# A Transformer layer with routed experts on one core: the experts' second layer by split products, and a score product moved

## The reference, cut to what matters

```python
x = x + attention(layernorm(x), Wq, Wk, Wv, Wo)     # x: 16 x 256 x 128, 16 heads, keys of 8, values of 64, causal
x = x + experts(layernorm(x), gate_w, w1, w2)       # 8 experts, capacity 64 tokens each per batch row

def experts(x, gate_w, w1, w2):
    probs = softmax(x @ gate_w)                      # B, T, 8
    top_p, top_idx = top_k(probs.transpose(0, 2, 1), 64)
    xin = gather(x, top_idx)                         # B, 8, 64, 128
    h = gelu(einsum('BElC,ECH->BElH', xin, w1))      # hidden width 512
    y = einsum('BElH,EHC->BElC', h, w2) * top_p[..., None]
    return zeros.at[b_idx, top_idx].add(y)
```

## Time and profile before

| | us |
|---|---|
| median of 3 runs | 535.61 |
| profiled execution | 535.0 |
| its span | 533.3 |
| PE busy | 512.2 (96%) |
| DVE busy | 422.5 (79%) |
| ACT busy | 401.3 (75%) |
| POOL busy | 264.6 (50%) |

### The profile page before, as it was taken

How to read it: one execution, slowest core, us unless ns; L and a number is a source line. 1 busy time by engine, 2 the same in 40 slices (tenths; PEclk the granted TensorE clock), 3 DMA queues, 4 the chain that set the end, 5 groups by cost and what they waited for, 6 DMA issues and landing times.

```text
span 533.3 us, 13983 instructions
## 1 busy us (share of the span) xinstructions
PE 512.2 (96%) x4783; PEld 424.8 (80%) x4783; DVE 422.5 (79%) x1081; ACT 401.3 (75%) x1379; POOL 264.6 (50%) x252
## 2 busy tenths in 40 slices
PE   3799999999999999999999999999999999999996
PEld 2477787887887877877877877867789998999996
DVE  6878898888888888889989999999974577634444
ACT  3799998999989899898989989899653644434330
...
DMA packets 49447, 45.71 MB, mean 86 GB/s; under 512 B 4208, under 2 KB 46192, under 8 KB 49392
## 3 DMA queue, kind: packets, MB, share of 16 engines
...
## 4 chain that ended last, share of the span: by engine, by line
PE 88%; DVE 5%; issue 2%; ACT 2%; DMA 1%; POOLq 0%; POOL 0%; ACTq 0%; DVEq 0%
PE ctx_ps L1266 16%; PE t_ps L1353 10%; PE misc_ps L1275 10%; PE t_ps L1239 5%; PE t_ps L1249 5%; PE t_ps L1240 5%; PE misc_ps L1177 4%; PE s_ps L1337 4%; PE misc_ps L1178 4%; PE misc_ps L1179 4%; PE s_ps L1225 3%; PE s_ps L1338 3%; PE s_ps L1339 3%; PE s_ps L1212 3%; PE s_ps L1221 2%
## 5 line engine op out<-in xcount | busy, mean ns | idle before, releaser
L580 ACT ACTIVATE prob<-s_ps,neg_max 128x128 f32<-128x128 f32 (+1 forms) x512 | 208.8, 426 | 2.7 <-DVE neg_max L1008 0.5
L504 POOL TENSOR_TENSOR probn<-prob,inv 128x1024 f32<-128x1024 f32 x64 | 121.3, 1895 | 53.0 <-DVE inv L1072 53.0
L580 ACT ACTIVATION_READ_ACCUMULATOR prob<-s_ps,neg_max 128x1 f32 x512 | 108.4, 212 | 0.0
L497 POOL TENSOR_TENSOR probn<-prob,inv 128x512 f32<-128x512 f32 x64 | 66.7, 1042 | 56.4 <-PE t_ps L1249 56.0
L628 ACT ACTIVATE hT<-s_ps 128x512 f32<-128x512 f32 x64 | 38.0, 598 | 64.4 <-PE s_ps L1339 61.8
L1008 DVE TENSOR_REDUCE neg_max<-s_ps 128x4 f32<-128x1024 f32 x63 | 75.1, 1193 | 0.8 <-PE s_ps L1225 0.8
L533 POOL TENSOR_TENSOR y_parts<-y_sb,y_parts 128x512 fp32r<-128x512 f32 x16 | 21.3, 1328 | 106.9 <-ACT y_parts L638 106.9
L1275 PE MATMUL misc_ps<-wo_sb,ctxT 128*128 128x128 f32 x512 | 67.8, 275 | 0.9 <-DVE x_all L827 0.9
L1275 PEld LDWEIGHTS misc_ps<-wo_sb,ctxT 128*128 128x128 f32 x512 | 62.2, 192 | 1.3 <-issue 1.3
L1239 PE MATMUL t_ps<-ident,probn 128*128 128x128 f32 x256 | 61.8, 281 | 0.0
L1240 PE MATMUL t_ps<-ident,probn 128*128 128x128 f32 x256 | 60.1, 275 | 0.0
...
## 6 DMA issues: line engine op xcount, KB each, us to landing
...
```

What stands on the lines that cost most here:

```text
L497: nc.gpsimd.tensor_tensor(probn[r][:, 0:HG * P].rearrange("p (i k) -> p i k", i=HG), prob[r][:, 0:HG * P].rearrange("p (i k) -> p i k", i=HG),
L504: nc.gpsimd.tensor_tensor(probn[r][:, HG * P:].rearrange("p (i k) -> p i k", i=HG), prob[r][:, HG * P:].rearrange("p (i k) -> p i k", i=HG ...
L580: last = nc.scalar.activation(prob[r][:, first + i * keys:first + (i + 1) * keys], scores[:, i, :], ACT.Exp, bias=neg_max[:, r, block_, i: ...
```

## The change: what it does

The second layer is made the other way round. The weights `w2` are now the stationary operand and are held as a pair (`w2_first_hi/lo`, `w2_rest_hi/lo`); the hidden layer is the moving operand (256 columns) and is a pair too (`h_hi`, `h_lo`). `expert_out(m, half)` is 12 fp32r matmuls for one expert of the pair; both halves of a pair fill the bank `misc_ps[1]`. The result stands with the channels on the partitions, so ACT copies it (`copy_y`) and four PE transposes (`turn_y`) turn it back to where it was before.

To get the pair of the hidden layer, ACT evaluates the gelu twice from PSUM, once into `h_raw` (float32) and once into `h_hi`; POOL subtracts for k = 0, 2 and 3 and DVE for k = 1 (`split_h`). The weights' pair is made for the experts 0 to 3 on POOL in the units 47 to 54 (a copy and a subtraction in turn), for the experts 4 to 7 by four ACT copies behind `copy_turned_late(63, 1)` and four POOL subtractions behind `split_w1`.

The loop's order is new: expert_out(n - 1, 1) stands where the whole of it stood, turn_y(n - 1) follows hidden(n, 3), and expert_out(n, 0) ends the step. split_y moves ahead of gelu(n, 1) but for n = 3, 4, 5; scale_y moves behind the rounds of the top-64 search in DVE's list; DVE splits the last y. In the attention units `first_scores` stands ahead of `values`. The stores of the result are written out instead of a loop, and the buffer for DMA descriptors is smaller.

```diff
+Y_SPLIT_AT = {3: 2, 4: 2, 5: 2}
+W2_UNITS = tuple(range(47, 55))
...
+        yT_ps = misc_ps[1][:, :].rearrange("p (h q s) -> p h q s", h=2, q=QB)
...
@@ POOL @@
+            def split_w2(e, step):
+                if step == 0:
+                    pool.wait_ge(w2_loaded, 16)
+                    nc.gpsimd.tensor_copy(w2_first_hi[:, e, :, :], w2_first[:, e, :, :]).then_inc(w2_hi_done, 1)
+                else:
+                    pool.wait_ge(w2_hi_done, e + 1)
+                    nc.gpsimd.tensor_tensor(w2_lo_of(e), w2_raw_of(e), f32(w2_hi_of(e)),
+                                            ALU.subtract).then_inc(w2_ready, 1)
+            def split_h(n, k):
+                pool.wait_ge(h_ready, 4 * n + k + 1)
+                await_count(pool, yT_done, 2 * n - 1 + k // 2)
+                nc.gpsimd.tensor_tensor(h_lo[:, k, :, :], h_raw[:, k % RING, :, :], f32(h_hi[:, k, :, :]),
+                                        ALU.subtract).then_inc(h_lo_ready, 1)
...
+                    if at(u, W2_UNITS):
+                        split_w2(*divmod(u - W2_UNITS[0], 2))
...
-            norm_scale(B - 1)
-            for m in range(B):
-                parts = y_parts[m // QB % RING]
...
+            for e in range(EP, E):
+                split_w2(e, 1)
+            for n in range(B + 1):
+                for k in range(4):
+                    if k == Y_SPLIT_AT.get(n, 1) and has(n - 2, B):
+                        split_y(n - 2)
+                    if n < B and k != 1:
+                        split_h(n, k)
+                    if n == 0 and k == 1:
+                        norm_scale(B - 1)
@@ ACT @@
             def gelu(n, k):
                 act.wait_ge(h_done, 4 * n + k + 1)
-                nc.scalar.activation(hT[n % RING][:, k // 2, 2 * (k % 2):2 * (k % 2) + 2, :],
-                                     h_ps[k % 2], ACT.Gelu).then_inc(h_ready, 1)
+                await_count(act, *((h_lo_ready, 3 * n - 1), (h_lo_ready, 3 * n), (h_lo_ready, 3 * n + 1), (h_lo1_ready, n + 1))[k])
+                nc.scalar.activation(h_raw[:, k % RING, :, :], h_ps[k % 2], ACT.Gelu)
+                await_count(act, yT_done, 2 * n - 1 + k // 2)
+                nc.scalar.activation(h_hi[:, k, :, :], h_ps[k % 2], ACT.Gelu).then_inc(h_ready, 1)
+            def copy_y(m):
+                act.wait_ge(yT_done, 2 * (m + 1))
+                await_count(act, y_done, m - 1)
+                nc.scalar.activation(y_turned[:, m % RING, :, :].rearrange("p q (h s) -> p h q s", h=2),
+                                     yT_ps, ACT.Copy).then_inc(yT_ready, 1)
...
             copy_turned_late(63, 1)
+            for e in range(EP, E):
+                split_w2(e)
             copy_xin(3)
...
-                        if k == 2 and has(m, B):
+                        if k == Y_SPLIT_AT.get(n, 1) and has(m, B):
                             split_y(m)
+                        if k == 2 and has(n - 1, B):
+                            copy_y(n - 1)
                         gelu(n, k)
@@ DVE @@
+            def split_h(n):
+                dve.wait_ge(h_ready, 4 * n + 2)
+                await_count(dve, yT_done, 2 * n - 1)
+                nc.vector.tensor_tensor(h_lo[:, 1, :, :], h_raw[:, 1, :, :], f32(h_hi[:, 1, :, :]),
+                                        ALU.subtract).then_inc(h_lo1_ready, 1)
...
                 for b in GATHERED_AT.get(n, ()):
                     take_gathered(b)
+                if 0 < n < B and n not in GATHERED_AMID:
+                    split_h(n)
...
                 m = n - 1
-                if has(m, B):
-                    scale_y(m)
...
                 for s in TOPS_BEHIND.get(n, ()):
                     top_round(1, s)
+                if has(m, B):
+                    scale_y(m)
+                if m == B - 1:
+                    split_last_y()
@@ PE @@
-            def expert_out(m):
-                pe.wait_ge(h_ready, 4 * (m + 1))
...
-                for q in range(QB):
-                    for c in range(HC):
-                        for half in range(2):
-                            last = nc.tensor.matmul(y_ps[half * CAP:(half + 1) * CAP, q, :],
-                                                    hT[m % RING][:, half, c, q * CAP:(q + 1) * CAP],
-                                                    w2_of(2 * (m % EP) + half)[:, c, :],
+            def expert_out(m, half):
+                e = 2 * (m % EP) + half
+                pe.wait_ge(h_lo_ready, 3 * m + (1, 3)[half])
+                if half == 0:
+                    pe.wait_ge(h_lo1_ready, m + 1)
...
+                for c in range(HC):
+                    hi, lo = [part[:, 2 * half + c // 2, c % 2, :] for part in (h_hi, h_lo)]
+                    for w, h in ((w2_hi_of, hi), (w2_hi_of, lo), (w2_lo_of, hi)):
+                        last = nc.tensor.matmul(misc_ps[1][:, half * QB * CAP:(half + 1) * QB * CAP], w(e)[:, c, :], h,
+                                                start=(c == 0 and h is hi and w is w2_hi_of),
+                                                stop=(c == HC - 1 and w is w2_lo_of))
+                last.then_inc(yT_done, 1)
+            def turn_y(m):
+                pe.wait_ge(yT_ready, m + 1)
...
                 for q in range(QB):
+                    last = nc.tensor.transpose(y_ps[:, q, :], y_turned[:, m % RING, q, :], ident[:, :])
                 last.then_inc(y_done, 1)
...
+                        await_count(pe, filled0, u + 2)
+                        first_scores((j + 2) % G, par if j < 2 else 1 - par)
+                    if has(u + 2, UNITS):
                         w, q = u + 2, (j + 2) % G
...
                         values(q, xb)
-                    if has(u + 2, UNITS):
-                        if j == 2:
-                            pe.wait_ge(qk_loaded, QK_LOADS * (b + 2))
-                        await_count(pe, filled0, u + 2)
-                        first_scores((j + 2) % G, par if j < 2 else 1 - par)
...
-                if has(n - 1, B):
-                    expert_out(n - 1)
+                expert_out(n - 1, 1)
+                if n == B:
+                    add_up(n - 5)
                 if has(n, B):
                     hidden(n, 2)
                     hidden(n, 3)
+                    turn_y(n - 1)
...
+                if n < B and has(n - 5, LAST):
+                    add_up(n - 5)
+                if has(n, B):
+                    expert_out(n, 0)
```

102 lines of the change are left out of this document (74 added, 28 removed).

## The result

The changed kernel takes 545.96 us (median of 4 runs, 543.72 to 547.00), the kernel before 535.69 (4 runs, 534.83 to 537.89): ratio 1.0186, 95% interval 1.0166 to 1.0206. It is 1.9% slower. 534.4 had been forecast, with a range up to 538.5: the prediction was wrong.

A forecast was written before the change was run, and what follows sets the result against it. PE was taken to set the time, with DVE and ACT close behind in attention. -7.0 - 1.0 + 3.3 + 1.1 + 1.0 + 1.4 = -1.2 on 535.0 gave 533.8, with 0.6 for the median 534.4 us; range 528.5 to 538.5.

The forecast's parts named there:

- Expert steps, PE: Expert steps 1 to 14: new second layer and transposes take 3.33 us instead of 3.83, gain 0.50 a step, -7.0 us.
- the 7.7 that the prediction named as a sign of being wrong: Expert steps: a step over 7.7 us would mean that GpSimd's four subtractions set the pace.
- Do the others keep up: Expert steps: ACT and GpSimd fit into a step except for a few waits of PE, together +1.1 us.
- DVE and GpSimd together: Expert steps 12 to 14: DVE, waiting for GpSimd's instructions, makes split_y and hidden late, +1.0 us.
- Tail, -1.0: From the last expert step to DVE's last addition: ends at T+17.1 instead of T+18.1, gain 1.0 us.
- Start, +3.3: Start of expert steps: GpSimd's four added subtractions delay DVE's picks and norm, so hidden(0, 2) starts 3.3 us later.
- Attention, +1.4: Attention units 47 to 54: an added GpSimd instruction a unit collides with DVE in six units, 0.23 us each on PE.
- rival 2: Attention units 47 to 54: each collision goes through to PE, 5.4 us instead of 1.4, giving 538.4; chance 0.25.
- Swap, 0: Attention units: first scores ahead of values gains nobody anything on the path, 0 us, bounds -3 and +2.
- Rival 4: Expert steps and start: the lock holds GpSimd too, 8.2 us against 7.2 in steps 12 to 14; 536.8; chance 0.10.

The follow-up runs named there:

- x1: Changed kernel, but from step 1 on GpSimd's three subtractions of the hidden activations cover only 16 of 256 columns of each half; 534.71 us.
- x15: Changed kernel with weight split in steps 0 to 2, later place tables, softmax heading step 3, y's subtraction on VectorE except steps 4 to 7; 539.33 us.
- x4: Changed kernel with the split of the second half of the second-layer weights moved from ahead of the expert steps into steps 0 to 2; 541.75 us.
- x17: x15 plus the fourth block's subtraction on VectorE, ahead of the remaining top rounds (steps 3, 4) and of the last place table (step 15); 534.07 us.
- x18: x17 with the attention's values ahead of the first scores again, as in the kernel before; 535.59 us.
- x6: Changed kernel with the values put back ahead of the first scores in an attention unit, the second layer staying changed; 545.42 us.
- x9: Changed kernel with the four place instructions of a row block merged into one and the two picks of a gather into one; 546.67 us.
- x13: Changed kernel with the subtraction of the second layer's output moved from GpSimd to VectorE, 15 times; 541.88 us.

## Why the prediction was wrong, point by point

- **"Expert steps, PE", -0.50 a step: right.** 0.47: steps 11, 12 and 14 run in 7.20. Step 13 took 8.65, over the 7.7 that the prediction named as a sign of being wrong, but not for the reason it gave: it was VectorE that came late, not GpSimd.
- **"Do the others keep up" and "DVE and GpSimd together", +1.1 and +1.0: the step that failed.** It measured 10.6 us. The place was right (VectorE's `place` and split_h beside GpSimd), the size was not. I counted GpSimd's time for itself (5.3 of 7.2 us) and gave VectorE the collisions in three steps only, as "nothing to 0.9 us". The row with a `pick` pair at 2.65 already said that the two take turns; then the times add. With GpSimd's 5.3, VectorE's subtraction of 0.69 and 1.13 for each four `place` that is 7.1 of 7.2 us in step 11 and, with the picks, 8.0 of 8.1 in steps 8 to 10, and none of these waited; it is 8.3 of 7.2 in steps 12 to 14, and TensorE waited 1.4 us in step 13 and again ahead of expert_out(15, 0). Steps 3, 4 and 7 were not worked out; they hold 8.6 of the 10.6. In steps 4 and 7 VectorE's list, lengthened by its turns, fills the step (busy 8.5 of 8.6 and 15.3 of 16.2 us). Step 3's 1.9 us stayed when GpSimd's subtractions were shrunk (x1) and fell to 1.0 when VectorE's softmax was moved (x15). The clock's fall behind the long wait of step 7 (1.6 us) wasn't thought of.
- **Tail, -1.0: wrong by 1.8.** The 0.8 us of waiting before expert_out(15, 1) was there, but expert_out(15, 0) waited 1.4 before it, for the same reason as in step 13; the other 0.4 us aren't located.
- **Start, +3.3: right** (3.2), by the mechanism named; x4 took 2.0 of it away.
- **A term was missing:** expert_out(0, 0) now runs ahead of step 1, 1.44 us. The tail was worked out without it, the sum should have been 535.9.
- **Attention, +1.4: wrong.** The collisions came in units 47 to 54 (two `xn` pairs took 1.0 us for 0.68, two `xg_lo` 1.03 for 0.42), but nothing of them reached TensorE: the contexts of before's 291.81 and 342.68 started at 292.26 and 343.13, 0.45 us later both times. In the profiles of the 13 versions with the same attention contexts(63) starts at 387.6 to 389.4, before at 388.17. So rival 2, the one that held the slower side, was wrong in place: the collisions that reached TensorE were those of the expert steps.
- **Swap, 0:** within its bounds; x17 against x18 shows 1.5 us of gain, x6 against the changed kernel none, and neither tells the swap's own share.
- **Rival 4** said that the lock holds GpSimd too, 536.8. The direction fits, its reading needed both halves: a short `place` costs GpSimd 0.1 to 0.2 us (1.45 and 1.46 for 1.30), less than its own 0.28, a merged one 0.7 to 1.0 (x9). This bears out, on VectorE's side plainly and on GpSimd's in part, what the Trainium skill (SBUF — State Buffer, "SBUF: two separate sides") says of an exclusive lock, also for VectorE instructions with two SBUF inputs: `h_lo` on VectorE took 1.65 to 1.76 where it waited for GpSimd, 0.69 free of it. The prediction weighed the rule and took only a tenth of a chance from it.

The scale is shown by x1: with 1/16 of each of GpSimd's `h_lo` 11.2 us go between the medians. In the profiled executions these are 8.1 of the 10.6 us in the steps and 2.5 behind them. x1 by itself also makes GpSimd's own results come sooner; that it is VectorE that was held is shown by its instructions' lengths and by x13, where VectorE does more and its `place` and `h_lo` get shorter. That GpSimd's share causes most of the loss is shown; which single collision costs what differs from version to version.
